# Layer 0's gate products one slot later, its second rows with them, and layer 1's projection bias added on VectorE

## What is computed

```
x = x + L0_xattn(layernorm(x), ctx)     # 16 heads of 64: q = x Wq, k = c Wk, v = c Wv,
                                        # softmax(q k / 8) v, then @ Wo + bo
x = x + L0_ffn(layernorm(x))            # (silu(x wg) * (x wu)) @ wd, hidden 768
x = x + L1_xattn(layernorm(x), ctx)     # as L0_xattn, other weights
x = x + L1_ffn(layernorm(x))            # rows quantised to int8, @ int8 rhs, scaled back
```

## Time and profile before

| what | value |
|---|---|
| time, three runs | 1689.70, 1693.38, 1697.56 us (median 1693.38) |
| time of the profiled execution | 1690.04 us |
| its span, first to last instruction | 1688.0 us |
| mean granted TensorE clock | 0.973 of full speed |
| busy: TensorE, VectorE, ScalarE, GpSimd | 93%, 81%, 77%, 73% of the span |

### The profile page before, as it was taken

The page is one execution under the profiler, slowest core; times in us unless marked ns, Lnnn a source line. Parts: engine busy times, 40 slices in busy tenths (PEclk is TensorE's granted clock), DMA queues, the critical chain, the costliest instruction groups (busy, mean ns, idle before and its releaser), DMA issues.

```text
span 1688.0 us, 75269 instructions
## 1 busy us (share of the span) xinstructions
PE 1568.0 (93%) x27538; PEld 1357.9 (80%) x27538; DVE 1364.3 (81%) x3490; ACT 1300.5 (77%) x5514; POOL 1232.4 (73%) x1966
## 2 busy tenths in 40 slices
PE   7999889999999999898999999999999999999995
PEld 4555578888888888888888889888888888888884
DVE  6777568787878778787878787788988988889886
ACT  6665678787877777787878777778888888888883
POOL 5120278787778787777877787778888888888884
PEclk9999999999999999999999999999999999999998
DMA  9998699867777777767676879879998888888995
GB/s 257 350 309 271 167 203 163 167 149 161 156 157 161 156 159 162 154 155 165 148 163 153 161 153 168 149 157 191 197 196 189 196 196 190 193 198 189 188 187 111
DMA packets 740023, 307.79 MB, mean 182 GB/s; under 512 B 629201, under 2 KB 725361, under 8 KB 737841
## 3 DMA queue, kind: packets, MB, share of 16 engines
q1 hardware_dynamic: 738049, 299.32, 81.1%
q0 software_dynamic: 1840, 6.82, 1.4%
HBM read 87.09 MB, written 65.54 MB: 90 GB/s over the span
## 4 chain that ended last, share of the span: by engine, by line
POOL 40%; issue 21%; PE 17%; DVE 5%; ACT 2%; DMA 2%; SPq 1%; POOLq 0%; DVEq 0%; ACTq 0%
POOL pr L1710 16%; PE psum L333 15%; POOL p L1723 11%; POOL p L1715 6%; POOL hT_l L1701 5%; POOL rs L395 2%; DMA pT<-p 2%; DVE sg L1515 2%; ACT th L1405 1%; DVE hf L1526 1%; PE psum L1278 1%; SPq L1129 1%; PE psum L1241 1%; DVE mv L384 1%; POOLq L274 0%
## 5 line engine op out<-in xcount | busy, mean ns | idle before, releaser
L1425 ACT ACTIVATE ex<-psum,nmax 128x77 f32<-128x77 f32 x2048 | 638.4, 340 | 21.2 <-DVE nmax L1550 15.1
L1425 ACT ACTIVATION_READ_ACCUMULATOR ex<-psum,nmax 128x1 f32 x2048 | 451.6, 221 | 0.0
L1715 POOL TENSOR_TENSOR p<-pr,p 128x308 f16<-128x308 f32 x512 | 386.9, 756 | 39.0 <-ACT p L348 0.6
L1710 POOL TENSOR_TENSOR pr<-ex,rden 128x308 f32<-128x308 f32 x512 | 373.8, 730 | 36.1 <-DVE rden L1555 36.0
L333 PE MATMUL psum<-xT,wq_h 128*64 128x256 f16 x4064 | 364.1, 281 | 0.0
L333 PE MATMUL psum<-xT,wq_l 128*64 128x256 f16 x2032 | 285.5, 277 | 0.0
L1550 DVE TENSOR_REDUCE nmax<-psum 128x4 f32<-128x308 f32 x512 | 238.1, 466 | 52.7 <-PE psum L1241 52.0
L1723 POOL CAST p<-pr 128x308 f16<-128x308 f32 x509 | 246.1, 483 | 40.8 <-DMA pT<-p 8.5
L333 PE MATMUL psum<-wo_h,oT_h 128*64 128x256 f16 x1792 | 251.4, 276 | 11.6 <-DVE oT_l L362 11.2
L333 PE MATMUL psum<-wo_l,oT_h 128*64 128x256 f16 x1792 | 250.0, 274 | 0.0
L333 PE MATMUL psum<-wo_h,oT_l 128*64 128x256 f16 x1792 | 250.0, 274 | 0.0
(11 more groups left out here) (172 smaller groups left out, 3604.1 us busy)
## 6 DMA issues: line engine op xcount, KB each, us to landing
keys<-ks SPq DMA_DIRECT2D x16, 1232.0 KB, 7.8
kb<-keys SPq DMA_DIRECT2D x256, 77.0 KB, 2.7
vb<-vals SPq DMA_DIRECT2D x128, 154.0 KB
vals<-vs SPq DMA_DIRECT2D x64, 256.0 KB, 4.2
x_pair<-in_x_dram SPq DMA_DIRECT2D x32, 256.0 KB, 3.0
pT<-p SPq DMA_TRANSPOSE x512, 3.3
x_res<-in_x_dram SPq DMA_DIRECT2D x32, 256.0 KB, 3.1
mid_x<-y SPq DMA_DIRECT2D x32, 256.0 KB, 2.6
```

Source lines behind the costliest of these rows:

```text
L1425: last = act.activation(ex[i][:, t, b, :], SC[:, t, b * NK:(b + 1) * NK], ACT.Exp, bias=nmax[i][:, t, b:b + 1], accum_out=den[i][:, t, b:b ...
L1710: pool.tensor_tensor(pr[:, t, :, :], ex[i][:, t, :, :], r, ALU.mult).then_inc(s_p, 1)
L1715: pool.tensor_tensor(d[:, t, 1, :, 0:NK], pr[:, t, :, :], d[:, t, 0, :, 0:NK], ALU.subtract).then_inc(s_pl, 1)
```

## The change

Chunks 0 and 1 move to slot 3, chunks 2 and 3 to slot 0 and chunks 4 and 5 to slot 1 of the next body, on all engines. `down(0)` goes behind the queries of slot 2. The second rows are normalised at the end of VectorE's slot 1 (before: end of slot 0), their low half is made in slot 2 (before: slot 1), and SyncE turns them in slot 2 behind both halves of P(1) (before: slot 1, between P(0,0) and P(0,1)). INV1 moves from GpSimd's slot 3 to the end of slot 0, INV0 from slot 1 to slot 2. In layer 1 the projection bias, four products a body on TensorE, becomes one VectorE addition to `x_res` in slot 2.

The diff, cut to its core (after's line numbers are a few lower: L1680s for L1690, L1707 for L1710):

```diff
@@ TensorE: project, and body
-                        if u == 1 - l:
-                            product(pe, OA[:, t, :], pick, bo_rows[:, l, :], True, start=False, stop=False,
+                        if u == 1 and l == 0:
+                            product(pe, OA[:, t, :], pick, bo_rows[:, :], True, start=False, stop=False,
...
                         if u == 0 and lay[-3] == 0:
+                            gate_up(2, bank("gu", 2))
+                        if u == 1 and lay[-3] == 0:
                             gate_up(4, bank("gu", 4))
                         if lay[0] is not None:
                             scores(n + u, u, 32 * (h + 1))
                         if u == 3 and lay[-2] == 0:
-                            gate_up(2, bank("gu", 2))
-                        if u == 2 and lay[-3] == 0:
-                            pe.wait_ge(s_hlp, len(LOW_POOL) * (h - 2))
-                            pe.wait_ge(s_hld, len(LOW_DVE) * (h - 2))
-                            down(0, bank("down", 0))
+                            pe.wait_ge(s_x2d, 16 * (h - 1))
...
+                            gate_up(0, bank("gu", 0))
...
+                        if u == 2 and lay[-3] == 0:
+                            pe.wait_ge(s_hlp, len(LOW_POOL) * (h - 2))
+                            pe.wait_ge(s_hld, len(LOW_DVE) * (h - 2))
+                            down(0, bank("down", 0))
                         if u == 0 and lay[-3] == 0:
+                            gate_up(3, bank("gu", 3))
+                        if u == 1 and lay[-3] == 0:
                             gate_up(5, bank("gu", 5))
@@ SyncE: body
-                        if u == 1 and lay[-2] == 0:
-                            turn_second_rows(h - 2)
                         if turning:
                             turn_probabilities(n + u - 1, (u - 1) % UNITS, 1)
+                        if u == 2 and lay[-2] == 0:
+                            turn_second_rows(h - 2)
@@ VectorE: body
+                        if u == 2 and lay[-3] == 0:
+                            low_hidden(4, h - 3)
...
+                        if u == 0 and lay[-3] == 0:
+                            sigmoid_gate(2, h - 3)
+                            hidden(2, h - 3)
+                        if u == 1 and lay[-3] == 0:
+                            sigmoid_gate(4, h - 3)
+                            hidden(4, h - 3)
+                        if u == 2 and lay[-2] == 0:
+                            dve.wait_ge(s_x216h, h - 1)
+                            low(dve, x216[:, :, 1, :], x2[:, :, :], x216[:, :, 0, :]).then_inc(s_x216l, 1)
...
+                        if u == 0 and lay[-3] == 0:
+                            low_hidden(1, h - 3)
+                        if u == 0 and lay[-2] == 0:
+                            dve.wait_ge(s_x1, h - 1)
+                            spreads(dve, x1[1 - odd], st2, s_st2)
+                        if u == 0 and lay[-2] == 0:
+                            moments(dve, 1, st2, mv2, ve2, s_st2, s_mv2, h - 2)
+                        if u == 0 and lay[-3] == 0:
+                            sigmoid_gate(3, h - 3)
+                            hidden(3, h - 3)
+                        if u == 1 and lay[-2] == 0:
+                            normalise_rows(dve, 1, x2, x1[1 - odd], mv2, rs2, h - 1, s_x2)
+                        if u == 1 and lay[-3] == 0:
+                            sigmoid_gate(5, h - 3)
+                            hidden(5, h - 3)
...
+                        if u == 2 and lay[-1] == 1:
+                            dve.wait_ge(s_xr, 16 * h)
+                            bias = bo_b[:, 1, :].unsqueeze(1).to_broadcast([P, QT, D])
+                            dve.tensor_tensor(x_res[:, :, :], x_res[:, :, :], bias, ALU.add).then_inc(s_xb, 1)
@@ GpSimd: body
                         if u == 0 and lay[-3] == 0:
+                            low_hidden(0, h - 3)
+                        if u == 1 and lay[-3] == 0:
                             low_hidden(2, h - 3)
+                        if u == 2 and lay[-3] == 0:
+                            low_hidden(5, h - 3)
...
-                        if u == 0 and lay[-3] == 0:
+                        if u == 1 and lay[-3] == 0:
                             low_hidden(3, h - 3)
+                        if u == 2 and lay[2] == 0:
+                            inverse(pool, 0, ve1, rs1, h + 2)
+                            shift(pool, 0, mv1, rs1, h + 2)
...
+                        if u == 0 and (lay[-2] == 0 or lay[-3] == 0):
+                            inverse(pool, 1, ve2, rs2, h - 1)
```

More of the change, by code:

```diff
@@ L1036, in uses @@
                 if u == 0 and lay[-3] == 0:
-                    out += [("gu", 4), ("gu", 5)]
+                    out += [("gu", 2), ("gu", 3)]
                 if u == 1:
+                    if lay[-3] == 0:
+                        out += [("gu", 4), ("gu", 5)]
                     if lay[1] == 1:
@@ L1042, in uses @@
                     if lay[-3] == 0:
[L1043 to L1049, removed]
+                        out += [("down", 0), ("down", 1)]
                     if lay[-2] == 1:
@@ L1452, in body @@
                         if u == 0 and lay[-3] == 0:
+                            tanh_gate(2, h - 3)
+                        if u == 1 and lay[-3] == 0:
                             tanh_gate(4, h - 3)
-                        if u == 1 and lay[-3] == 0:
-                            high_hidden(4, h - 3)
                         if lay[(u + 1) // UNITS] is not None:
@@ L1557, in body @@
                     for u in range(UNITS):
-                        if u == 0 and lay[-2] == 0:
-                            dve.wait_ge(s_x1, h - 1)
-                            spreads(dve, x1[1 - odd], st2, s_st2)
                         if u == 3 and lay[-3] == 0:
@@ L1568, in body @@
                             maxima(n + u, u % 2, 0)
-                        if u == 0 and lay[-2] == 0:
-                            moments(dve, 1, st2, mv2, ve2, s_st2, s_mv2, h - 2)
                         if lay[-1] is not None:
@@ L1588, in body @@
                                                      op1=ALU.subtract).then_inc(s_kvf, 1)
-                        if u == 3 and lay[-2] == 0:
-                            low_hidden(1, h - 2)
-                        if u == 0 and lay[-3] == 0:
-                            sigmoid_gate(4, h - 3)
                         if u == 2 and lay[2] == 0:
@@ L1679, in body @@
                             spreads(dve, y, st3, s_st3)
-                        if u == 2 and lay[-2] == 0:
-                            sigmoid_gate(1, h - 2)
-                        if u == 2 and lay[-2] == 0:
-                            hidden(1, h - 2)
                         if u == 3 and lay[-1] is not None:
                             dve.wait_ge(s_oa, h)
-                            dve.wait_ge(s_xr, 16 * h)
+                            if lay[-1] == 0:
+                                dve.wait_ge(s_xr, 16 * h)
+                            else:
+                                dve.wait_ge(s_xb, h - B)
                             after(dve, s_x2, QT * (h - 1))
@@ L1723, in probabilities @@
                         pool.tensor_copy(p16[v % 2][:, t, 0, :, 0:NK], pr[:, t, :, :]).then_inc(s_ph, 1)
-                        if between is not None:
-                            low_hidden(*between)
                         low_of(b, v, t)
@@ L1748, in body @@
                             probabilities(h, u, 0)
-                        if u == 1 and lay[2] == 0:
-                            inverse(pool, 0, ve1, rs1, h + 2)
-                            shift(pool, 0, mv1, rs1, h + 2)
+                        if u == 0 and (lay[-2] == 0 or lay[-3] == 0):
+                            inverse(pool, 1, ve2, rs2, h - 1)
                         if u == 2 and lay[-3] == 0:
@@ L1754, in body @@
                             shift(pool, 2, mv3, rs3, h - 2)
-                        if u == 2 and lay[-2] == 0:
-                            low_hidden(0, h - 2)
-                        if u == 3 and lay[-1] is not None:
+                        if u == 3 and lay[-1] == 1 and lay[-2] == 1:
                             inverse(pool, 1, ve2, rs2, h)
```

105 lines of the change are left out of this document (38 added, 67 removed).

## The result

The changed kernel took 1757.09 us (median of 4 runs, 1756.78 to 1763.00), the kernel before 1695.47 us beside it (4 runs). The ratio is 1.0376, with a 95% interval of 1.0339 to 1.0413: slower by 3.8%, and 3.1 us from the forecast of 1754. The profiled execution took 1756.78 us, span 1754.7.

The account below looks back on a forecast made before the run. Layer 0 was taken as a ring of waits through GpSimd, TensorE and VectorE. 1690.04 + 64.5 - 1 - 3 = 1750.5 us profiled, with 3.3 for the median 1754 us, 3.6% slower; range 1712 to 1800.

Parts of the forecast that it names:

- LH5: GpSimd's last low half in layer 0, which `down(0)` needs; forecast to end 16.0 us after slot 0's scores start.
- P(1,1): GpSimd's last whole P of the layer 0 body; forecast to end 18.35 us after slot 0's scores start.
- the first wait: TensorE at `down(0)` in layer 0, idle until GpSimd's last low half: 3.5 us, against 1.29 before.
- The company of VectorE and GpSimd: Layer 0: VectorE's low-half work running beside GpSimd's steps stretches them; 0.5 us added.
- The term of 31 bodies: Layer 0: 31 bodies going from 27.22 to 29.3 us each, +64.5 us.
- Body h = 2 loses two gate products, about -1; the last bodies keep their length: Bodies at the change of layers: h = 2 gains about 1 us, the last ones stay unchanged.
- the 3.3 added for the median: Whole kernel: the profiled execution before was 3.3 us below the median of runs, so 1750.5 became 1754.
- A fall costs little: Layer 0: a clock fall behind the first wait slows work that waits for `x2T` anyway, eating up the second wait.
- the second wait: TensorE at `gate_up(0)` in layer 0, waiting for the second rows' transfer to `x2T`: 1.7 us, new.
- The rival by which the clock falls on the path in every body: Layer 0: a fall behind `x2T` costs each body 1.7 us more, 31 us; about 1807 us; chance 0.10.
- Layer 1: Bias products leave TensorE for a VectorE addition: 0.1 x 28 = -3 us, between -6 and +2.
- Even slots win: Rival: layer 0's body is TensorE's work alone, about 24.2 us; about 1597 us, faster; chance 0.09.

Follow-up runs that it names:

- turn_early: The changed kernel with the second rows turned (`x2T`) ahead of P(1,1)'s turning in SyncE's queue: 1708.2 us, ratio 1.0090.
- down_front: The changed kernel with `down(0)` back ahead of the queries in slot 2, as in the kernel before: 1806.08 us, ratio 1.0676.
- lh5_ring: both_early with LH5 ahead of P(1,0) on GpSimd, and `x2T` back behind P(1,1)'s turning: 1759.57 us, ratio 1.0392.
- x2_first: both_early with LH5 ahead of P(1,0) on GpSimd, and `x2T` ahead of both turnings of slot 2: 1645.19 us, ratio 0.9730.
- lh4_first: x2_first with chunk 4's low half ahead of the values' low half on VectorE in slot 2: 1645.83 us, ratio 0.9723.
- both_early: The changed kernel with `x2T` ahead of P(1,1)'s turning and the first reciprocals of slots 0 and 1 earlier on VectorE: 1685.87 us, ratio 0.9967.

## Why the prediction was right, and where it was off

- **Mechanism: right.** The changed kernel's layer 0 is longer because LH5 and `x2T` come late, LH5 by GpSimd's order behind VectorE's reciprocals, and `x2T` by SyncE's order behind P(1,1), which the same reciprocals hold. Each was shown: `x2T` issued earlier alone gave 49 us back, the reciprocal earlier alone 34, LH2 and INV1 earlier alone 33; with the waits down to 1.1 and 1.0 us 96 came back, with 1.1 and none 112. These gains hold fewer falls of the clock too (2 and none against 22). With the first wait nearly taken away and the second left, nothing came back (1759.6), since the second grew and the falls came onto the path.
- **The steps**, counted from S0 = 440.14, forecast and found: P(0,0) ended at 8.35 and 8.1; LH2 at 9.7 and 9.5; P(1,0) started at 13.1 and 12.8; LH5 ended at 16.0 and 15.6; P(1,1) at 18.35 and 18.1; `down(0)` waited 3.5 and 3.03; `gate_up(0)` waited 1.7 and 1.53 and started at 23.15 and 22.7; the body took 29.3 and 28.7. No step was wrong in kind; VectorE's list up to the first reciprocal was about 0.2 us shorter than summed from single rows, and GpSimd's steps followed; the transfer and what follows it took another 0.3 less.
- **The company of VectorE and GpSimd**, an allowance of 0.5: LH5 took 0.85 instead of about 0.7 and P(1,1)'s multiply 1.14 instead of 0.70, together 0.6. That multiply ran beside VectorE's subtraction of 0.76 us. By the rule of the Trainium skill cited in the prediction (SBUF — State Buffer, section "SBUF: two separate sides") the loser would be blocked for the rest of that subtraction, 0.58 us; the rows show 0.44, somewhat less.
- **The sum came out by two errors that cancel.** The term of 31 bodies was set at 64.5 us and measured 59.2. Inside it, 27 bodies had a mean of 28.9 instead of 29.3, 10 us less than forecast; the last four of the 31, h = 30 to 33, took 29.3, 30.2, 33.3 and 29.3, 5 us more. The terms around it were too small: body h = 2 was to gain 1 us and lost 5.5 (`gate_up(0)` waited 3.89 us there, and the clock fell), and h = 34 took 30.5 against 25.3 before. So the bodies at the change of layers do not keep their length: h = 31 to 33 took 26.2, 26.2 and 26.4 before. Where the two layers' steps mix, TensorE waits 1.4 us for `hf` and up to 3.0 for `x2T`. Much of both losses hangs on the place of `x2T` in SyncE's queue: in turn_early h = 2 took 23.8 us, as before the change, and h = 31 to 33 took 27.8 each, though h = 34 still took 29.0. The part of the prediction that failed is "Body h = 2 loses two gate products, about -1; the last bodies keep their length". That the total came within 3.1 us is thus in part luck. For the profiled execution the sum was 6.2 us too low (1750.5 against 1756.8); the 3.3 added for the median hid half of that, while this kernel's profiled execution lay only 0.3 below its median.
- **A fall costs little: right.** Most bodies with one took 28.7 to 28.85 us in the changed kernel, since it shortens the second wait. turn_early showed the other side: with no second wait a fall costs 1.55 us. The rival by which the clock falls on the path in every body did not hold for the change, but two edits of it came to that: down_front, in front of slot 3, and lh5_ring, at and behind `x2T`, where the rival had it.
- **Layer 1: right in size.** 0.14 to 0.16 us a body were gained, forecast 0.1. But the total of the rest of the kernel rose by 1.7 us, since h = 34 lost 5.2.
- **Even slots win** was rejected rightly for this order, and its condition named the two steps that mattered: with LH5 and `x2T` early the same slots gave 1645 us. But it was not enough. LH5 ended at 12.8 in x2_first, and then TensorE waited for chunk 4's low half on VectorE; with that gone too, in lh4_first, waits of 0.1 to 0.6 us at three or four places left the body at 25.95 us. The 1597 us of that rival, a body that is TensorE's work alone, was not reached by any kernel.

## What to carry over

When work is moved to even out one engine, follow the longest chain of the other engines' program orders through the new places before counting the evened engine's gain; here it kept all its work (24.2 us a body) and waited 4.5 us in it instead of 2.1. A step put behind another in a transfer queue or a list costs what the one ahead waits for, so put what is ready first ahead: one transposing transfer moved by one place was worth 49 us, and 98 us in another order, the falls of the clock included. Once a wait is removed, read the clock again: some of the gain, or loss, lies in it.

## What the runs showed that was not expected

- The number of clock falls is not in proportion to the waiting. TensorE was busy 24.2 of 26.3 us in the kernel before, with 19 falls in 31 bodies, and 24.2 of 25.9 in x2_first, with none. In the one, waits of 0.7 to 0.8 us (for an exponential) and 0.8 to 1.3 us (at `down(0)`) stand close together in slot 2; in the other, waits of 0.6 and 1.1 us lie 12 to 14 us apart. What decides is not shown: both_early, with one wait of 2.1 us a body, had 16 falls, and turn_early, with one of 3.0, had 14. Of the 1.40 us that a body gained between the kernel before and x2_first (27.22 to 25.82), 19 x 1.6 / 31 = 0.98 are the falls (bodies of 27.9 instead of 26.3 us), and only 0.4 the shorter steady body. The Trainium skill (TensorE: Matmul & The Clock Gate, section "HAM oscillation — how this bites in real kernels") describes a loop in which the wait of each round drops the clock. down_front, with a wait of 4.46 us and a fall in every body, agrees. The kernel before has falls in over half of its bodies with the shorter waits above.
- A fall can be free: in the changed kernel it lay in front of a wait for a transfer. A second one in the same body is not (30.0 us).
- Removing a wait can bring no gain at all while its twin stands: lh5_ring took 2.4 us of waiting from `down(0)` and ended within its interval of the changed kernel (1.0392 against 1.0376). The other wait grew by 1.4 us, and 36 pieces of fall, now on the path, stand against 22 that were mostly covered.
